# Cross-attention on one core: output tiles in sequence, the range check between the norms, and a whole-array first key chunk and first Q

## The reference

```python
Q = x @ W_Q          # x: 1024 x 128, W: 128 x 1024, 16 heads of 64
K = ctx @ W_K        # ctx: 6404 x 128
V = ctx @ W_V
scores = einsum('hqd,hkd->hqk', Q, K) / sqrt(64)
attn = softmax(scores)
context = einsum('hqk,hkd->hqd', attn, V)
out = context @ W_O + x
out = (out - mean(out)) / sqrt(var(out) + 1e-5)      # per row
```

## Time and profile before

| | us |
|---|---|
| median of 3 runs | 1628.64 (1628.42 to 1628.89) |
| the profiled execution | 1629.81 |
| its span | 1627.9 |
| PE busy with matmuls | 1612.7 (99%) |
| DVE busy | 1210.3 (74%) |
| ACT busy | 955.5 (59%) |
| POOL busy | 58.8 (4%) |

### The profile page before, as it was taken

One profiled execution on the slowest core, in us unless ns is written; L12 is line 12 of the kernel. 1 busy time (PEld: TensorE's weight loads), 2 busy tenths in 40 slices (PEclk: granted clock), 3 DMA queues, 4 the chain that ended last, 5 costly groups with the idle time before them and its releaser, 6 DMA issues.

```text
span 1627.9 us, 39517 instructions
## 1 busy us (share of the span) xinstructions
PE 1612.7 (99%) x17422; PEld 643.8 (40%) x17422; DVE 1210.3 (74%) x1214; ACT 955.5 (59%) x1064; POOL 58.8 (4%) x38
## 2 busy tenths in 40 slices
PE   9999999999999999999999999999999999999997
PEld 3443344333443334433344333443344433444334
DVE  5778787787877778777787777778777787777876
ACT  5556565655556656565655656555665565655652
POOL 0000000000000000000000000000000000000100
PEclk9999999999999999999999999999999999999998
DMA  4000000000000000000000000000000000000000
GB/s 159 2 2 8 2 8 2 1 8 2 8 2 2 8 1 9 2 1 9 1 9 2 2 8 2 9 2 2 8 1 9 2 8 2 2 9 2 8 2 14
DMA packets 12366, 13.76 MB, mean 8 GB/s; under 512 B 4512, under 2 KB 8096, under 8 KB 12192
## 3 DMA queue, kind: packets, MB, share of 16 engines
q1 hardware_dynamic: 11760, 10.61, 2.0%
q10 hardware_dynamic: 432, 0.59, 0.1%
HBM read 10.36 MB, written 0.59 MB: 7 GB/s over the span
## 4 chain that ended last, share of the span: by engine, by line
PE 98%; DVE 1%; DMA 0%; ACT 0%; issue 0%; SPq 0%; ACTq 0%
PE o_ps L374 43%; PE s_ps L357 43%; PE w_ps L421 6%; PE w_ps L404 5%; PE s_ps L444 0%; DMA ctx_all<-in_ctxT 0%; PE o_ps L444 0%; PE w_ps L444 0%; ACT probs L538 0%; DVE sums L637 0%; DVE k_all L625 0%; DVE y L731 0%; DVE limits L741 0%; DVE y L714 0%; PE o_ps L421 0%
## 5 line engine op out<-in xcount | busy, mean ns | idle before, releaser
L637 DVE TENSOR_TENSOR sums<-sums,probs 128x1024 f32<-128x1024 f32 (+1 forms) x800 | 997.6, 1247 | 376.4 <-ACT probs L538 372.3
L538 ACT ACTIVATE probs<-s_ps 128x1024 f32<-128x1024 f32 x816 | 834.9, 1023 | 639.5 <-PE s_ps L357 621.4
L357 PE MATMUL s_ps<-q_sb,k_all 64*64 64x512 f32 x6528 | 847.9, 589 | 0.8 <-DVE q_sb L625 0.6
L374 PE MATMUL o_ps<-probs,v_all 64*64 64x512 f32 x6528 | 847.7, 589 | 0.0
L357 PEld LDWEIGHTS s_ps<-q_sb,k_all 64*64 64x64 f32 x6528 | 251.1, 133 | 449.9 <-issue 447.0
L374 PEld LDWEIGHTS o_ps<-probs,v_all 64*64 64x64 f32 x6528 | 246.8, 133 | 390.8 <-issue 385.5
L404 PEld LDWEIGHTS w_ps<-wv_sb,ctx_all 64*64 64x64 f32 x3232 | 97.2, 133 | 57.6 <-issue 51.8
L421 PE MATMUL w_ps<-ctx_all,wk_sb 64*64 64x512 f32 (+1 forms) x832 | 107.1, 585 | 0.5 <-DMA ctx_all<-in_ctxT 0.5
L404 PE MATMUL w_ps<-wv_sb,ctx_all 64*64 64x128 f32 x3232 | 106.9, 269 | 0.4 <-DVE k_all L625 0.4
L625 DVE TENSOR_TENSOR k_all<-k_all,w_ps 128x512 f32<-128x512 f32 (+1 forms) x104 | 69.6, 670 | 6.8 <-ACT k_all L546 6.8
L332 POOL TENSOR_TENSOR o_b<-o_a,o_b 128x512 f32<-128x512 f32 x15 | 31.5, 2097 | 1116.2 <-ACT o_a L568 1116.2
(11 more groups left out here) (59 smaller groups left out, 104.8 us busy)
## 6 DMA issues: line engine op xcount, KB each, us to landing
inv_sum<-inv_dram SPq DMA_DIRECT2D x30, 128.0 KB, 2.8
ctx_all<-in_ctxT SPq DMA_DIRECT2D x12, 256.0 KB, 5.6
quad_rows<-quad_sums SPq DMA_DIRECT2D x60, 4.0 KB, 1.7
xT_sb<-in_xT ACTq DMA_DIRECT2D x2, 256.0 KB, 4.6
x_sb<-in_x SPq DMA_DIRECT2D x1, 512.0 KB, 10.1
wo_sb<-in_wo SPq DMA_DIRECT2D x1, 512.0 KB, 11.1
out<-y SPq DMA_DIRECT2D x4, 128.0 KB, 1.8
wq_sb<-in_wq SPq DMA_DIRECT2D x1, 448.0 KB, 6.9
```

The costliest lines, as they stand in the source:

```text
L357: last = nc.tensor.matmul(s_ps[part(half), u % 2, head * QH:(head + 1) * QH], k_all[part(head), c * P + half * DH:c * P + (half + 1) * DH] ...
L374: last = nc.tensor.matmul(o_ps[part(head), rows, :], v_all[part(rows), c, part(head)], probs[part(rows), u % RING, head * QH:(head + 1) * QH],
L538: nc.scalar.activation(probs[:, u % RING, :], s_ps[:, u % 2, :], ACT.Exp, scale=SCALE).then_inc(probs_ready, 1)
L637: nc.vector.tensor_tensor(out=sums[0:rows, t % 2, :], in0=sums[0:rows, t % 2, :], in1=probs[0:rows, u % RING, :], op=ALU.add).then_inc(sum ...
```

## The change

- The warm-up is four matmuls of 256 columns instead of two of 512.
- FIRST becomes: the first chunk of 128 keys of K ("a"), Q half 0, the other 384 keys of K block 0, V block 0. The first two (WHOLE) use the whole array, 128 rows by 128 columns, so their results are complete: ACT copies one part out and DVE another, side by side (`pieces_of`), with no addition. The scores of unit 0 stand between K block 0 and V block 0 on PE; on ACT the exponential of unit 0 stands ahead of V's half. DVE's order is as before: all pieces of FIRST, then the sums.
- The context's first block is loaded in two DMAs (128 columns, then 384), and xT's second half is issued by SP behind context block 1, not by ACT.
- At the end PE makes tiles 4 to 7 one after the other, with all their pairs; the count for the range check stands between tiles 6 and 7. DVE makes the range check between the second and the third group of the layer norm.
- The read of the choice (`load_choice`) is separated from the branch. SP reads it between its second and its third store; the other engines read it where they did, at the end of their work.

```diff
-    WARM_UP = 2
+    WARM_UP = 4
-    FIRST = [("k", 0, 0), ("q", 0, 0), ("v", 0, 0)]
+    FIRST = [("a", 0, 0), ("q", 0, 0), ("k", 0, 0), ("v", 0, 0)]
+    WHOLE = FIRST[:2]
...
         def banks_of(found):
-            if found == FIRST[1]:
+            if found == FIRST[0]:
+                return [s_ps[:, 1, 0:QH], s_ps[:, 1, 0:QH]]
+            if found in (FIRST[1], FIRST[3]):
                 return [o_ps[:, 0, :], o_ps[:, 1, :]]
-            if found == FIRST[2]:
-                return [s_ps[:, 1, 0:QH], s_ps[:, 1, QH:2 * QH]]
             return [w_ps[:, 0, :], w_ps[:, 1, :]]
+        def first_key(found):
+            return P if found == FIRST[2] else 0
+        def pieces_of(found):
+            one, two = banks_of(found)
+            if found == FIRST[0]:
+                return one[part(0), 0:P], k_all[part(0), 0:P], two[part(1), 0:P], k_all[part(1), 0:P]
+            w = QH // 2
+            return one[:, 0:w], q_sb[:, 0, 0:w], two[:, 0:w], q_sb[:, 0, w:QH]
...
-        def if_general(eng, program):
+        def load_choice(eng):
             eng.wait_ge(choice_ready, 1)
-            chosen = eng.value_load(use_general[0:1, 0:1], min_val=0, max_val=1)
+            return eng.value_load(use_general[0:1, 0:1], min_val=0, max_val=1)
+        def if_general(eng, chosen, program):
             with eng.If(chosen > 0):
                 program()
...  SP
-            load_ctx(0)
+            sp.dma_start(ctx_all[:, 0:P], ctxT[:, 0:P]).then_inc(chunk_loaded, 16)
+            sp.dma_start(ctx_all[:, P:BK], ctxT[:, P:BK]).then_inc(ctx_loaded[0], 16)
             sp.dma_start(wv_sb[:, 0:2 * DH], w_v[:, 0:2 * DH]).then_inc(first_w_loaded["v"], 16)
-            for b in range(1, BLOCKS):
+            load_ctx(1)
+            sp.dma_start(xT_sb[:, QH:NQ], xT[:, QH:NQ]).then_inc(x_loaded[1], 16)
+            for b in range(2, BLOCKS):
                 load_ctx(b)
...
-            store(0)
+            store(0, (0, 1))
+            chosen = load_choice(sp)
+            store(0, (2, 3))
             sp.wait_ge(stored, 16 * (QT // 2))
-            if_general(sp, general_and_store)
+            if_general(sp, chosen, general_and_store)
...  PE, scores(u)
                 if u == 0:
                     pe.wait_ge(work_ready, COUNT["q", 0, 0])
-                if u == 1:
-                    pe.wait_ge(work_ready, COUNT["v", 0, 0])
+                    pe.wait_ge(work_half, COUNT["q", 0, 0])
...
-                if c % BLOCK == 0 and h == 0:
+                if u == 1:
+                    pe.wait_ge(work_ready, COUNT["k", 0, 0])
+                if u > 0 and c % BLOCK == 0 and h == 0:
                     pe.wait_ge(work_ready, COUNT["k", pair, c // BLOCK])
...  PE, work(found)
+                if kind == "a":
+                    pe.wait_ge(first_w_loaded["k"], 16)
+                    pe.wait_ge(chunk_loaded, 16)
+                    nc.tensor.matmul(banks[0][:, 0:P], wk_sb[:, 0:P], ctx_all[:, 0:P],
+                                     start=True, stop=True).then_inc(work_done, 1)
+                    return
+                if found in WHOLE:
+                    pe.wait_ge(first_w_loaded["q"], 16)
+                    pe.wait_ge(x_loaded[0], 16)
+                    for n in range(2):
+                        last = nc.tensor.matmul(banks[n][:, 0:QH // 2], wq_sb[:, 0:P],
+                                                xT_sb[:, n * (QH // 2):(n + 1) * (QH // 2)], start=True, stop=True)
+                    last.then_inc(work_done, 1)
+                    return
+                if found == FIRST[3]:
+                    pe.wait_ge(work_half, COUNT["q", 0, 0])
+                    pe.wait_ge(work_ready, COUNT["q", 0, 0])
...
             for _ in range(WARM_UP):
-                nc.tensor.matmul(s_ps[0:DH, 0, 0:QH], ones[:, :], o_a[:, :], start=True, stop=True)
-            for found in FIRST:
+                nc.tensor.matmul(s_ps[0:DH, 0, 0:QH // 2], ones[:, :], o_a[:, 0:QH // 2], start=True, stop=True)
+            for found in FIRST[:3]:
                 work(found)
-            for u in range(AHEAD):
-                scores(u)
+            scores(0)
+            work(FIRST[3])
+            scores(1)
...
-            for t in (4, 5):
-                project_output(t, range(PAIRS - 1))
+            project_output(4, range(PAIRS - 1))
+            pe.wait_ge(last_norm_done, 1)
+            project_output(4, [PAIRS - 1]).then_inc(y_done, 1)
+            project_output(5, range(PAIRS)).then_inc(y_done, 1)
             pe.wait_ge(work_ready, COUNT["d", PASSES - 1, 0])
-            for t in (6, 7):
-                project_output(t, range(PAIRS - 1))
-            pe.wait_ge(last_norm_done, 1)
-            for t in range(QT // 2, QT):
-                project_output(t, [PAIRS - 1]).then_inc(y_done, 1)
-            pe.wait_ge(y_taken, QT)
+            project_output(6, range(PAIRS)).then_inc(y_done, 1)
+            pe.wait_ge(y_taken, 2)
             pe.wait_ge(exact_ready, 1)
             nc.tensor.matmul(s_ps[0:1, 0, 0:1], exact[:, :], ones[:, 0:1], start=True, stop=True).then_inc(exact_counted, 1)
+            project_output(7, range(PAIRS)).then_inc(y_done, 1)
...  ACT
-            for h in range(NQH):
-                act.dma_start(xT_sb[:, h * QH:(h + 1) * QH], xT[:, h * QH:(h + 1) * QH]).then_inc(x_loaded[h], 16)
-            for found in FIRST:
+            act.dma_start(xT_sb[:, 0:QH], xT[:, 0:QH]).then_inc(x_loaded[0], 16)
+            for found in FIRST[:3]:
                 take_half(found)
-            for u in range(AHEAD):
-                exps(u)
+            exps(0)
+            take_half(FIRST[3])
+            exps(1)
...  DVE, add_half(found)
+                if found in WHOLE:
+                    _, _, mine, target = pieces_of(found)
+                    dve.wait_ge(work_done, COUNT[found])
+                    nc.vector.tensor_copy(target, mine).then_inc(work_ready, 1)
+                    return
...
             dve.wait_ge(xres_loaded, 32)
-            layer_norm(0)
+            layer_norm(0, (0, 1))
...  the range check, L740 to L758, unchanged
+            layer_norm(0, (2, 3))
```

More of the change, by code:

```diff
@@ L145, in cross_attention_kernel @@
         xres_loaded = sem("xres_loaded")
+        chunk_loaded = sem("chunk_loaded")
         ctx_loaded = [sem(f"ctx_loaded{i}") for i in range(BLOCKS)]
@@ L209, in banks_of @@
         def banks_of(found):
-            if found == FIRST[1]:
+            if found == FIRST[0]:
+                return [s_ps[:, 1, 0:QH], s_ps[:, 1, 0:QH]]
+            if found in (FIRST[1], FIRST[3]):
                 return [o_ps[:, 0, :], o_ps[:, 1, :]]
-            if found == FIRST[2]:
-                return [s_ps[:, 1, 0:QH], s_ps[:, 1, QH:2 * QH]]
             return [w_ps[:, 0, :], w_ps[:, 1, :]]
+        def first_key(found):
[6 more added lines that the diff above has]
+            return one[:, 0:w], q_sb[:, 0, 0:w], two[:, 0:w], q_sb[:, 0, w:QH]
         def target_of(found):
             kind, at, b = found
+            if kind == "a":
+                return k_all[:, 0:P], P
             if kind == "k":
-                return k_all[:, b * BK:b * BK + cols_in(b)], cols_in(b)
+                skip = first_key(found)
+                return k_all[:, b * BK + skip:b * BK + cols_in(b)], cols_in(b) - skip
             if kind == "v":
@@ L301, in general, with store @@
                 g_loops(sp, load_weights, g_nothing, load_blocks)
-            def store(turn):
-                for n in range(QT // 2):
+            def store(turn, groups):
+                for n in groups:
                     sp.wait_ge(ln_done, QT * turn + 2 * n + 2)
@@ L309, in general_and_store @@
                 general()
-                store(1)
+                store(1, range(QT // 2))
                 sp.wait_ge(stored, 2 * 16 * (QT // 2))
             out_t = out.rearrange("(t p) d -> p t d", p=P)
-            store(0)
+            store(0, (0, 1))
+            chosen = load_choice(sp)
+            store(0, (2, 3))
             sp.wait_ge(stored, 16 * (QT // 2))
-            if_general(sp, general_and_store)
+            if_general(sp, chosen, general_and_store)
         @block.gpsimd
@@ L412, in work @@
                             weights = wk_sb[part(rows), at * P + head * DH:at * P + (head + 1) * DH]
-                            moving = ctx_all[part(rows), b * BK:b * BK + cols_in(b)]
+                            moving = ctx_all[part(rows), b * BK + first_key(found):b * BK + cols_in(b)]
                         elif kind == "q":
@@ L526, in general @@
                     project_output(t, range(PAIRS)).then_inc(y_done, 1)
-            if_general(pe, general)
+            if_general(pe, load_choice(pe), general)
         @block.scalar
@@ L545, in take_half @@
                 act.wait_ge(work_done, COUNT[found])
-                nc.scalar.activation(target, banks_of(found)[0][:, 0:n], ACT.Copy).then_inc(work_half, 1)
+                mine = banks_of(found)[0][:, 0:n]
+                if found in WHOLE:
```

(22 more changed lines are left out.)

1 line of the change is left out of this document (added).

## The result

| | before | after |
|---|---|---|
| median, us | 1628.89 (1628.42 to 1629.27, 8 runs) | 1624.03 (1622.99 to 1624.52, 8 runs) |
| ratio | | 0.9969 (0.9958 to 0.998) |
| profiled execution, us | 1629.81 | 1624.32 |
| its span, us | 1627.9 | 1622.2 |

The change makes the kernel faster by 0.3%, 4.9 us here and 5.1 to 5.5 us in three later comparisons. Forecast were 1622.0 us and a range up to 1623.8: right side, right places, 2.0 us too good (1.8 in the difference, since before's median is 0.25 us higher here), and the measured median lies 0.2 us outside the range.

The account below looks back on a forecast made before the run. PE bounds the kernel (98% of the chain), so only start and end can gain: span 1627.9 - 5.95 - 0.7 = 1621.25, profiled execution 1623.15, median 1622.0 us; range for 8 in 10: 1621.0 to 1623.8.

Parts of the forecast that it names:

- Where the end is set: Last 5.1 us of the span, outside the chain: PE's branch (3.83 us) sets the end, hidden after the change.
- rival C: At the end PE's branch becomes the bound: 5.7 us long gives 1623.7, 7.5 us gives 1625.4; chance 0.10.
- PE and DVE in the tail: Tiles 4 to 6 end at 1614.56, the range check fills DVE's hole, the norm ends at 1619.6 against 1620.39.
- PE's own tail: From choice to meeting 4.8 us: starts at 1616.6 (late end) or 1615.0 (early end), span ending 1621.7 or 1620.1.
- The bound of -5.0 us: Smallest gain of the end's term: a store that takes 2.4 us and a branch 0.6 us longer.
- The store's landing: Last store at the end: issued at 1619.6, lands 1.8 us later at 1621.4; 2.4 us in the bound.
- The term of the end: Span end moves from 1627.9 to 1621.95: -5.95 us, bounds -5.0 and -6.3.
- The start: scores(0) at 8.15 instead of 9.80, V block 1 at 15.44 instead of 16.14: -0.7 us, bounds -1.4 and +0.8.
- Q wait for xT: At the start xT's half, issued at 1.18, lands 4.6 us later at 5.78; PE starts Q at 5.92.
- The scale: Span to median: 1.9 us around the span added, then 1.17 taken off, as before's median lies below its profiled execution.
- The rule against the change: Whole-array weight loads in Q at the start stay open, costing 0.45 to 0.9 us; part of rival B, chance 0.18 with its opposite.

Follow-up runs that it names:

- end_only: Only the changed end, with the start of before, against before at 1629.24 us: 1624.18 us, ratio 0.997 (0.9957 to 0.9982).
- after_again: The changed kernel timed once more, nothing altered, against before at 1629.24 us: 1623.74 us, ratio 0.9968 (0.9956 to 0.998).
- start_only_again: Only the changed start, with the end of before, timed a second time against before at 1629.07 us: 1628.49 us.

## Why the prediction was right and wrong, point by point

**Where the end is set: right.** The 5.1 us that the chain doesn't show were PE's branch, and it is hidden now. Its duration was 3.4 to 4.0 us over the profiles, so rival C (5.7 us) did not come up. The Trainium skill has the reason (Runtime: NRT & Kernel Launch, Instruction fetch mechanics: a taken branch out of the fetched window must wait for a fetch). The trace agrees: a packet of q8 lies inside PE's branch (at 1616.1 us, in 1614.5 to 1618.5), and ACT, DVE and SP with their short programs branched in 0.05 to 0.07 us.

**PE and DVE in the tail: right.** Tiles 4 to 6 ended 5.36 us after 1607.94 (5.37 in the sum), PE waited for nothing, and from tile 6's end at 1613.30 to the norm's at 1618.17 it took 4.9 us, against 5.0 forecast. As to PE's own tail, its early end was the true one. The bound of -5.0 us added a late store and a longer branch, though the two run side by side; with the prediction's own numbers they give -5.35.

**The store's landing: the step that failed.** The sum took 1.8 us "from issue to landing" from the earlier trace rows, and 2.4 as the worst. It took 3.5 in this profile, 1.7 us more, and 3.0 on the mean of the changed kernel's four profiles, 1.2 more. The experiments tie the excess to the instruction fetches beside it. I had asked what runs beside the branch (rival C: "now stores run beside it") but only what the store does to the branch, not what the branch's fetches do to the store, which was last in the chain. The sign was in before's trace: one store took 2.4 us, and it was the one with a q8 packet just ahead of it (1612 to 1613 us). The term of the end was then 1622.2 - (1627.9 - 1.24) = -4.5 us in the profile and -5.1 in the times of `end_only`, against -5.95.

**The start: right in its main mechanism, its size too sure.** Copies side by side took 0.38 and 0.42 us (0.40 forecast), scores(0) to V block 1 took 7.08 (7.29), DVE's sums stood back to back, PE waited 1.05 us before V block 1 (1.1). V block 1 came at 14.90, 0.54 earlier than forecast: 0.33 since scores(0) came earlier, as the clock rose in the middle of Q and not at 7.3, and 0.21 on the way from there, where ACT's exponential followed scores(0) by 0.93 us and not 1.16. I had read one profile's rise as a property of the kernel. Its times say -0.5 us, not the -0.7 of the sum.

One step was right by luck. The sum has Q wait for xT until 5.92, and Q did start at 5.93. But xT landed 3.3 us after its issue at 1.18, by 4.5; what Q stood behind was "a", which took 0.73 us at the lower clock and not 0.45. Where PE rose within the warm-up, "a" took 0.42 and Q started at 5.22. The other keys of K took 0.81 us in the chain and not 0.65.

**The scale: a second step that failed.** The profiled execution of before was 1.17 us above the median, and I took that off the changed kernel too. That profile was one with a late rise; the changed kernel's was only 0.3 us above its median. In the span the sum was 0.95 us low: 1.7 for the store, less 0.54 for the start and some 0.2 for the norm. In the median it was 2.0 low, and the other 1.1 are this offset (0.9) and the time outside the span (0.2). With the store at its mean of 3.0 us and not 1.8, the forecast would have been 1623.2, inside its range; the scale did the rest.

**The rule against the change: not borne out.** At the full clock whole-array Q took 0.86 to 0.87 us (`after_again`, `start_only_again`), as long as the four quarters. Q's length leaves no room for a weight load in the open, and that the start gave less than its forecast in time did not come from there.

**The chances.** No rival was what happened: it was a cost that none of them named. A range worked out from one profile should have held the effect of the clock's rise (1.5 us at V block 1) and a landing beyond the largest of four.

## What to carry to other kernels

Read branches, register reads and the meeting by source line wherever the span ends later than the chain; if a long branch is last, make its condition early and let it run beside other work. Then ask what the branch fetches, during it and for some us behind it, and what is in flight then: here it was worth 0.4 to 0.8 us to keep PE's fetches off the last store by branching later, while holding back ACT and DVE cost more than it gave. Where a start is costed from one profile, look first at whether PE's level there is the same in other executions.

## What the runs showed of the hardware

- Instruction fetches share the DMA engines with data: beside a store of 128 KB they moved its landing from 1.8 to 2.1 us to 2.4 (packets of q14, 0.01 MB each, alone), 2.9 (one of q8, 0.02 MB, alone) and 2.8 to 3.5 us (both).
- PE's branch is followed by a fetch of its own: in the changed kernel one q8 packet starts 1.6 us into the branch and another 3.1 us later, 0.7 us after the branch ended.
- With ACT's and DVE's branches held until the stores were in, the time outside the span rose from 2.2 to 3.3 and 3.8 us; that it is the fetch put off is argued from where its packets lie.
- PE's passage from 1.2 to 2.4 GHz at the start came anywhere from some 4.4 to 7.6 us after the span's start with the same instructions before it, and in the one profile with the hole of 0.48 us filled it came at some 7.3, as in before. These points are estimates from durations, since the column of the granted clock reads 1.00 throughout.
- PE reads a register and starts a branch while matmuls issued earlier are still queued: the read began at 1613.6, tile 7's matmuls ran until 1615.4.
